# Up projections as Strassen products over pairs of chunks, with prepared weights kept in DRAM

## Time and profile before

| | |
|---|---|
| median of 3 runs | 1947.38 us (1946.74 to 1948.69) |
| the profiled execution's own time | 1943.46 us |
| its span in the trace | 1941.6 us |
| PE busy | 1844.0 us (95% of the span), 8256 matmuls |
| DVE, ACT, POOL busy | 1040.9 us (54%), 523.4 us (27%), 347.8 us (18%) |
| mean granted TensorE clock | 0.99 |
| moved by DMA | 66.39 MB, mean 34 GB/s |

### The profile page before, as it was taken

The page is one execution under the profiler, slowest core; times in us unless marked ns, Lnnn a source line. Parts: engine busy times, 40 slices in busy tenths (PEclk is TensorE's granted clock), DMA queues, the critical chain, the costliest instruction groups (busy, mean ns, idle before and its releaser), DMA issues.

```text
span 1941.6 us, 21968 instructions
## 1 busy us (share of the span) xinstructions
PE 1844.0 (95%) x8256; PEld 1513.5 (78%) x8256; DVE 1040.9 (54%) x1598; ACT 523.4 (27%) x833; POOL 347.8 (18%) x318
## 2 busy tenths in 40 slices
PE   6799999999999999999999999999999788899998
PEld 5578888888887888788888888887777566677876
DVE  7653333333336565633333333367566579966676
ACT  4322112111214432321211121133333223322221
POOL 1100000000003110000000000002455462145464
PEclk9899999999999999999999999999999998999999
DMA  7400000000000000001000001000011000000002
GB/s 260 156 1 33 33 33 32 0 32 32 27 5 1 1 1 1 33 33 33 19 14 32 32 4 39 32 33 3 32 44 38 23 33 1 33 34 34 17 34 88
DMA packets 34754, 66.39 MB, mean 34 GB/s; under 512 B 2160, under 2 KB 10736, under 8 KB 32752
## 3 DMA queue, kind: packets, MB, share of 16 engines
q1 hardware_dynamic: 26224, 61.04, 8.7%
...
## 4 chain that ended last, share of the span: by engine, by line
PE 76%; DVE 11%; issue 5%; POOL 5%; ACT 2%; DMA 0%; DVEq 0%; POOLq 0%; SPq 0%; ACTq 0%
PE work L313 18%; PE work L315 18%; PE work L317 13%; PE acc L313 9%; PE acc L317 9%; PE acc L315 7%; POOL x L989 3%; DVE stats L1075 1%; PE work L451 1%; DVE xT_lo L1156 1%; DVE w_lo L1217 1%; DVE hid L1171 1%; DVE waiting L1130 1%; DVE scaled L1194 1%; ACT hid_hi L774 1%
## 5 line engine op out<-in xcount | busy, mean ns | idle before, releaser
L313 PE MATMUL work<-xT_hi,w_hi 128*128 128x512 f32 (+1 forms) x1760 | 692.2, 393 | 26.0 <-issue 10.8
L315 PE MATMUL work<-xT_lo,w_hi 128*128 128x512 f32 (+1 forms) x1760 | 688.6, 391 | 0.0
L317 PE MATMUL work<-xT_hi,w_lo 128*128 (+1 forms) x1056 | 412.6, 391 | 0.0
L313 PEld LDWEIGHTS work<-xT_hi,w_hi 128*128 128x128 f32 x1760 | 332.4, 189 | 97.6 <-issue 18.1
L313 PE MATMUL acc<-w_hi,hid_hi 128*128 128x512 f32 x936 | 370.8, 396 | 25.8 <-DVE scaled L1194 11.7
L315 PEld LDWEIGHTS work<-xT_lo,w_hi 128*128 128x128 f32 x1760 | 332.4, 189 | 71.6 <-issue 3.4
L1171 DVE SCALAR_TENSOR_TENSOR hid<-work,hid 128x512 f32<-128x512 f32 x128 | 88.5, 692 | 532.0 <-ACT hid L771 532.0
L317 PE MATMUL acc<-w_hi,hid_lo 128*128 128x512 f32 x936 | 366.6, 392 | 0.0
L989 POOL TENSOR_TENSOR x<-x,scaled 128x512 f32<-128x512 f32 x188 | 264.4, 1439 | 204.7 <-DVE scaled L1194 168.9
L771 ACT ACTIVATE hid<-work 128x512 f32<-128x512 f32 x128 | 76.6, 598 | 717.2 <-PE work L317 717.2
L1174 DVE TENSOR_TENSOR hid_lo<-hid,hid_hi 128x512 fp32r<-128x512 f32 x216 | 183.3, 849 | 151.0 <-ACT hid_hi L774 151.0
...
## 6 DMA issues: line engine op xcount, KB each, us to landing
...
```

Of the source, the lines that this page charges most:

```text
L313: pe.matmul(out, a_hi, b_hi, start=start, stop=False, skip_group_check=onto)
L315: last = pe.matmul(out, a_hi, b_lo, start=False, stop=stop and zero == "a", skip_group_check=onto)
L317: last = pe.matmul(out, a_lo, b_hi, start=False, stop=stop, skip_group_check=onto)
```

## The change

The up projections work on a pair of chunks (1024 tokens) at a time. For a **unit** (one block of gate rows and one of linear rows; for S the two blocks of B), the 2x2 product of [gate; up] x [two halves of the features] with [two halves] x [two chunks] is formed from seven products instead of eight, in the variant of Strassen's method with shared sums. Each product is two feature slices x three matmuls (two if exact). Names: p1, p5, p6, p2, p7, p3, p4, in PE's order; five PSUM banks hold BX, BY, BZ, BW and BV, and three (`RING`) take turns for down products and transposes.

- The sums on the weights' side (`w13_sums`) are made and split once, in pass 0 for A and in pass 1 for B and S, written to DRAM (`w13_kept`, 1.84 MB a unit; `w2_kept`, 0.52 MB a block) and loaded by SP for each unit from pass 1 on.
- The sums on the tokens' side (`sums`, four) and their split into seven operands (`convert`) are made once for each pass. `xc_hi` and `xc_lo` exist once: an operand is converted when the last unit of the pass before has used it.
- The sums behind the products go through PSUM: ACT copies BX to BY (`seed_y`) before p6 adds to it, ACT keeps p5 in SBUF (`keep_p5`), DVE writes BZ = BY + p5 (`seed_z`) before p3, ACT copies BY to BW after p7 (`seed` of BW, in ACT's slot) before p4, DVE writes BV = BY + p5 (`sum_c22`).
- The outer loop is over ten **passes** (layer, pair of chunks), and inside over units, called slots (`run`). Down products of a group stand between the first four and the last three products of the one or two slots after it; those of the last group (eight tiles) stand alone behind the last unit, in `tail`.
- B's down products are summed in SBUF (`y`) by DVE, not by GpSimd. The last group adds onto banks that ACT has filled with `y` (`seed`), DVE scales them, and `finish` adds them to x at the start of the pass after. The S layer's D * x moves from DVE and PSUM to GpSimd.
- One flag, read once before the first B pass, decides for all B passes. No engine's program has loops.

```diff
--- before.py
+++ after.py
...
+PASSES = [("A", 0, 0), ("A", 0, 1), ("A", 2, 0), ("A", 2, 1), ("B", 3, 0), ("B", 3, 1),
+          ("S", 4, 0), ("S", 4, 1), ("B", 5, 0), ("B", 5, 1)]
...
+W_OF = {"p1": 1, "p5": 3, "p6": 4, "p2": 2, "p7": 5, "p3": 6, "p4": 0}
+X_OF = {"p1": 0, "p5": 1, "p6": 2, "p2": 3, "p7": 4, "p3": 5, "p4": 6}
+
+BX, BY, BZ, BW, BV, RING = 0, 1, 2, 3, 4, 5
...
+    w13_kept = nc.dram_tensor("w13_kept", [W13_BASE["S"] + 1, P, 2 * 7 * 2 * P], F32).ap()
...
+            def w13_load(ps, s):
+                u = ps.u0 + s
...
+                if u >= 2:
+                    sp.wait_ge(p4_done, u - 1)
+                sp.dma_start(w13[:, u % 2, :, :].rearrange("p a n -> p (a n)").bitcast(F32),
+                             w13_kept[W13_BASE[ps.kind] + s]).then_inc(w13_in[u % 2], 16)
...
+            def prepared_out(s):
+                n = UNITS["A"] + s
+                sp.wait_ge(w13_ready, n + 1)
+                if s + 1 < UNITS["B"]:
+                    flat_load(t["gate"][s + 1], t["up"][s + 1])
+                elif s < UNITS["B"]:
+                    flat_load(t["b"][0], t["b"][1])
+                sp.dma_start(w13_kept[n], prep13[:, :, :].rearrange("p a n -> p (a n)").bitcast(F32)).then_inc(kept13[n % 2], 16)
...
-            def up(w, pair, c, buf, b, matrices, exact=False):
-                pair_wait(w)
-                for m in range(matrices):
-                    for k in range(KD):
-                        at = slice(b * D + k * P, b * D + (k + 1) * P)
-                        last = three(pe, work[:, 2 * pair + m, :], w_hi[buf][:, m, at], w_lo[buf][:, m, at],
-                                     xT_hi[:, c, k, :], xT_lo[:, c, k, :], k == 0, k == KD - 1,
-                                     "a" if exact else None)
-                last.then_inc(pair_full, 1)
...
+            def product(u, name, b, start, exact, first, done):
+                if first is not None:
+                    pe.wait_ge(xc_ready, conv_done(first) + X_OF[name] + 1)
+                for k in range(2):
+                    ws = slice((2 * W_OF[name] + k) * P, (2 * W_OF[name] + k + 1) * P)
+                    last = three(pe, bank(b), w13[:, u % 2, 0, ws], w13[:, u % 2, 1, ws], xc_hi[:, X_OF[name], k, :],
+                                 xc_lo[:, X_OF[name], k, :], start and k == 0, k == 1, "a" if exact else None, not start)
+                last.then_inc(done, 1)
...
+            def first_half(ps, s, exact):
+                u, first = ps.u0 + s, ps if s == 0 else None
+                if ps.no == 0:
+                    pe.wait_ge(w13_ready, s + 1)
+                else:
+                    pe.wait_ge(w13_in[u % 2], nth(u - passes[1].u0, 2))
+                if ps.no == BEFORE_T and s == 0:
+                    pe.wait_ge(t_free, len(t_use))
+                if u:
+                    pe.wait_ge(c11_read, u)
+                else:
+                    pe.wait_ge(fw_out, 16)
+                product(u, "p1", BX, True, exact, first, p1_done)
+                if u:
+                    pe.wait_ge(c22_read, u)
+                if ps.no == BEFORE_T and s == 0:
+                    pe.wait_ge(att_added, CH * TT)
+                if u == 0:
+                    pe.wait_ge(turned, PT)
+                product(u, "p5", BV, True, exact, first, p5_done)
+                pe.wait_ge(y_seeded, u + 1)
+                product(u, "p6", BY, False, exact, first, p6_done)
+                product(u, "p2", BX, False, exact, first, p2_done)
...
+            def second_half(ps, s, exact):
+                u, first = ps.u0 + s, ps if s == 0 else None
+                pe.wait_ge(z_seeded, u + 1)
+                product(u, "p7", BY, False, exact, first, p7_done)
+                product(u, "p3", BZ, False, exact, first, p3_done)
+                pe.wait_ge(w_seeded, u + 1)
+                product(u, "p4", BW, False, exact, first, p4_done)
...
+                onto = ps.kind == "B" and g == len(ps.groups) - 1
+                if onto:
+                    pe.wait_ge(seeded, PT * {3: 0, 5: 2}[ps.li] + PT * ps.pair + i + 1)
+                else:
+                    bank_free("d", d)
...
+            def run(ps, exact=False):
+                for s in range(ps.n):
+                    first_half(ps, s, exact)
+                    for g, i, d in ps.downs[s]:
+                        down(ps, g, i, d, exact)
+                    turn_tiles(ps, s)
+                    second_half(ps, s, exact)
+                for g, i, d in ps.downs[ps.n]:
+                    down(ps, g, i, d, exact)
+                turn_tiles(ps, ps.n)
...
+            def convert(ps, m):
+                act.wait_ge(sums_ready, 4 * (ps.no + 1))
...
+                else:
+                    act.wait_ge(freeing[m], ps.u0)
+                copy(xc_hi[:, m, :, :], sources[m], AF.Copy).then_inc(xc_hi_ready, 1)
...
+            def seed_y(u):
+                act.wait_ge(p1_done, u + 1)
+                if u:
+                    act.wait_ge(c22_ready, u)
+                copy(bank(BY), bank(BX), AF.Copy).then_inc(y_seeded, 1)
...
+            def keep_p5(u):
+                act.wait_ge(p5_done, u + 1)
+                if u:
+                    act.wait_ge(hid_ready, plan.lo_no[u - 1, 0, 1])
+                copy(sg[:, 1, :], bank(BV), AF.Copy).then_inc(p5_kept, 1)
...
+            def seed(ps, i, d):
+                user = plan.free_by["d", d]
+                act.wait_ge(freed[user[0]], user[1] + 1)
+                act.wait_ge(added, d - PT + 1)
+                copy(bank(plan.ring["d", d]), y[:, i, :], AF.Copy).then_inc(seeded, 1)
...
+            def tail(ps):
+                following, m = follower(ps), 4
+                for g, i, d in ps.downs[ps.n]:
+                    if ps.kind == "B":
+                        seed(ps, i, d)
+                    if following and m < 7:
+                        convert(following, m)
+                        m += 1
...
+            def sums(ps, step):
+                b11, b12, b21, b22, t2 = (xs[:, n, :, :] for n in range(5))
+                if step == 0:
+                    dve.wait_ge(turned, turns_before(ps.no + 1))
+                    tt(b12, b22, b12, ALU.subtract).then_inc(sums_ready, 1)
+                elif step == 1:
+                    dve.wait_ge(sums_ready, 4 * ps.no + 1)
+                    tt(t2, b12, b11, ALU.add).then_inc(sums_ready, 1)
+                elif step == 2:
+                    dve.wait_ge(sums_ready, 4 * ps.no + 2)
+                    if ps.no == 6:
+                        dve.wait_ge(skip_done, PT)
+                    tt(xn[:, 0:2, :], b22, t2, ALU.subtract).then_inc(sums_ready, 1)
+                else:
+                    tt(xn[:, 2:4, :], b21, t2, ALU.subtract).then_inc(sums_ready, 1)
...
+            def w13_sums(n):
+                dve.wait_ge(flat_in, 32 * (n + 1))
+                link(tt(flat[:, 4, :], flat[:, 0, :], flat[:, 1, :], ALU.add))
+                tt(flat[:, 6, :], flat[:, 2, :], flat[:, 0, :], ALU.subtract)
+                link(tt(flat[:, 5, :], flat[:, 4, :], flat[:, 2, :], ALU.subtract))
+                tt(flat[:, 7, :], flat[:, 3, :], flat[:, 5, :], ALU.subtract).then_inc(flat_ready, 1)
...
+            def seed_z(u):
+                dve.wait_ge(p6_done, u + 1)
+                dve.wait_ge(p5_kept, u + 1)
+                if u:
+                    dve.wait_ge(c12_read, u)
+                tt(bank(BZ), bank(BY), sg[:, 1, :], ALU.add).then_inc(z_seeded, 1)
...
+            def sum_c22(u):
+                dve.wait_ge(w_seeded, u + 1)
+                tt(bank(BV), bank(BY), sg[:, 1, :], ALU.add).then_inc(c22_ready, 1)
...
+            def gated(ps, s):
+                u = ps.u0 + s
+                scale = up_s[:, s:s + 1] if ps.kind == "B" else 1.0
+                dve.wait_ge(c12_read, u + 1)
+                dve.wait_ge(c22_ready, u + 1)
+                nc.vector.scalar_tensor_tensor(sg[:, 1, :], bank(BV), scale, sg[:, 1, :], ALU.mult,
+                                               ALU.mult).then_inc(c22_read, 1)
+                dve.wait_ge(c11_read, u + 1)
+                dve.wait_ge(p4_done, u + 1)
+                nc.vector.scalar_tensor_tensor(sg[:, 0, :], bank(BW), scale, sg[:, 0, :], ALU.mult,
+                                               ALU.mult).then_inc(c21_read, 1)
+                low(u, 0, 1, sg[:, 1, :])
+                low(u, 0, 0, sg[:, 0, :])
...
+            def slot(ps, s):
+                u, following, last = ps.u0 + s, follower(ps), ps.no == len(passes) - 1
+                seed_z(u)
+                if ps.no == 0 and s + 1 < UNITS["A"]:
+                    w13_split(s + 1)
+                if s == 0:
+                    finish(ps)
+                m = 0
+                for g, i, d in ps.downs[s]:
+                    add_tile(ps, g, i, d)
+                    if following and s == ps.n - 1:
+                        convert(following, m)
+                        m += 1
+                if ps.no == 0:
```

(48 more changed lines are left out.)

1932 lines of the change are left out of this document (993 added, 939 removed).

## The result

The changed kernel takes 1983.29 us (median of 4 runs, 1979.9 to 1987.43), the kernel before in the same session 1947.06. The ratio is 1.0186, 95% interval 1.0164 to 1.0208: 36 us slower. The forecast was 1959, 12 us slower, with a range that holds the result.

The account below looks back on a forecast made before the run. PE was taken to set the time. New costs less old waits, 141 us, against 130 saved gave +11: 1955 on the profiled 1943.46, and 1959 us as median. Range 1895 to 2010, the forecast's own 1940 to 1990.

Parts of the forecast that it names:

- What was removed: Up projections in A, B and S: 572 fewer matmuls at 0.2267 us each, 129.7 us saved.
- The wait in a B unit: Exact B: p6 starts 4.4 us after p7's end, matmuls cover 3.63; 0.75 us per unit, 33 us over 44.
- The rival in which this chain closes: B units: p7's end to p6 takes 3.6 us or less, B's 33 us go, total 1926; chance 0.34.
- Ends of passes: Last down tiles stand uncovered behind the last unit: 14 us over four A passes, 32 us in B.
- S: The two S passes: open chain, DVE's queue and cold restarts leave PE idle, 54 us.
- start: Before pass 0's first product: p1 at 102 us instead of 85.1, +17 us, bounds 8 and 25.
- starts of passes: First slots: statistics on DVE ahead of `seed_z`, also weight sums and first operands in pass 0; A 8 us, B 22.
- the section on waits in a unit: Chain from p7 to the next unit's p6: no wait in A, where 24 matmuls take 5.44 us; 33 us in B.
- transfers: Pass 1's loads and stores just fit beside PE at 398 GB/s; 5 us taken for the 12 units.
- the rival in which transfers bound pass 1: Pass 1: at 300 GB/s a unit takes 18.3 us instead of 15.2, total 1991; chance 0.10.
- restarts: After long idle gaps in S, PE restarts at the 1.2 GHz clock: four gaps, 7 us, inside S's 54.
- attention priced at +4: Attention: conversions for pass 2 behind the last attended tile, 2.3 us, and last softmax without transposes to fill it, 2.

Follow-up runs that it names:

- no_seeds: Changed kernel without the three copies that carry partial sums between PSUM banks, so outputs lack those sums: 1929.47 us, ratio 0.9909.
- p7_split: Changed kernel with p7 behind two of a slot's down tiles instead of four, DVE and ACT orders adapted: 1995.35 us, ratio 1.0248.
- combined2: Changed kernel with many queue reorderings from single runs together, plus repairs to pass 1's attention tiles and B's second statistics: 1914.74 us, ratio 0.9827.
- pass_ends: Changed kernel with two instead of four of DVE's input conversions ahead of a pass's last C22 sum, the others later: 1976.85 us, ratio 1.0138.
- flat_first: Changed kernel with SP, in pass 0, issuing the next raw up weights' load ahead of the wait for W2's split: 1967.59 us, ratio 1.0102.
- no_affine: Changed kernel without three of ACT's four scaling operations per tile transposed in pass 1, so attention's inputs lack them: 1974.87 us, ratio 1.0134.
- warm_fill: Changed kernel with 396 added matmuls that nobody reads filling PE's longest waits, no order changed: 1977.79 us, ratio 1.0150.

## Why the prediction was wrong in size

**What was removed** is right to the matmul: 7684 at a distance of 0.2267 us.

**The wait in a B unit** is right in mechanism and close in size. PE, ACT and DVE around one:

```profile
1409.43 0.39 PE L357 MATMUL psum<-xc_hi,w 128*128 128x512 f32 x1
1409.63 0.58 ACT L950 ACTIVATE psum<-psum 128x512 f32<-128x512 f32 x1 [3.85 <-PE psum L359]
...
1410.46 0.69 DVE L1323 TENSOR_TENSOR psum<-psum,sg 128x512 f32<-128x512 f32 x1
...
1411.25 0.69 ACT L953 ACTIVATE sg<-psum,small 128x512 f32<-128x512 f32 x1 [1.04 <-DVE psum L1323]
...
1411.97 0.75 DVE L1330 SCALAR_TENSOR_TENSOR sg<-psum,small,sg 128x512 f32<-128x512 f32 x1 [0.82 <-ACT sg L953]
...
1412.78 0.50 PE L357 MATMUL psum<-xc_hi,w 128*128 128x512 f32 x1 [0.42 <-DVE sg L1330]
...
1413.93 0.50 PE L357 MATMUL psum<-xc_hi,w 128*128 128x512 f32 x1
```

p7's slot is over at 1409.43. The copy from PSUM to PSUM takes 0.58 us (0.60 taken), p5 starts after 3.35 us, p6 after 4.50 (4.4 forecast) where 16 matmuls take 3.63. A slot is 10.8 us without other work on DVE and 11.0 with an input sum, for 10.75 forecast. The rival in which this chain closes needed 0.75 us less; with the seeds gone (no_seeds) or p7 earlier (p7_split, combined2) it does close, so the rival named the right lever.

**Ends of passes.** Before the B tails PE waits 6.09 us (6.2 forecast), in A 3.8, 2.7, 3.1, 3.1 (3.4). pass_ends shows the cause, DVE's conversions.

**S** is 51 us for 54, its waits 10.3, 13.2, 5.6, 3.6, 8.2 and 1.5 for 10.8, 12.9, 5.4, 6.1, 7.7 and 3.9. The **start** was too dear by 5 us.

**The first step that failed: the weight preparation of pass 0 priced at nothing but its first slots.** The term "starts of passes" gave pass 0 3.1 us for statistics and weight sums and 1.2 for first operands, and the section on waits in a unit said of A "no wait". That compared the length of one chain with PE's work. It did not follow the queues: of the extra 26 us, flat_first returns 13 (16 in the total) by issuing one load earlier. The other 12 or so stay open: in flat_first's pass 0 PE still has waits of 3.3, 2.8 and 1.3 us on DVE in its first slots. PE was held by an add, which was behind a split, which was behind ACT's split, which was behind a load, which was behind SP's wait for something else. SP's program shows this order before anything runs; each DMA of a moved step has to be placed in time against the wait in front of it.

**The second: pass 1's slots with attention tiles.** The term for it held 5 us for transfers and 3 for DVE. Transfers cost next to nothing. From 400 to 540 us:

```profile
400.00:540.00 140.00, 140.00 (x610) 113.55 (x609) 99.04 (x150) 78.68 (x120) 0.00 (x0) 1.00 0.93 364
```

PE is busy without a gap at a DMA share of 0.93 (0.9 forecast) and 364 GB/s, and the slots are 15.2 us. The 364 GB/s are 2% above the figure of 358 GB/s that the Trainium skill's page DMA: Bandwidth & Descriptors, under Specifications, gives for a core; the rival in which transfers bound pass 1 is refuted. The 0.2 us above the 15.0 of passes 2 and 3 are a hand-over at C22's gate (starts 0.29 and 0.34 us apart in place of 0.23), not a load. What was missed is ACT: two tiles a slot with 4.1 us of scaling and splitting in front of the seed of W, 1.2 to 1.5 us of wait in each of five slots (no_affine: 8 us).

**The third: restarts.** The forecast put 7 us for the lower clock, in S alone. The rows that are 0.43 us apart add up to 39.0 us for 14.0 before: they stand behind long waits at the ends and starts of passes and in attention too, most at 1.2 to 2.6 us apiece. warm_fill got 10 of them back. Beside that, the short waits cost more than they show: of the 1.0 us that a B slot of 11.0 is too long, the rows show 0.42 as wait; the rest is the first matmul after it, the hand-over to p6 and matmuls begun late.

**The fourth: attention priced at +4.** It lost 16. The forecast had the two ends: the wait for the first conversion is 2.1 us (2.3 taken), the last softmax wait 1.5 (2 taken). It had nothing for the start and the middle. PE's recorded waits, without the one for the conversion, are 17.4 us for 7.3 before: 5.1 and 0.5 for the first softmax, 4.2 twice for the second norm's output (L886), 3.4 for low parts, the 1.5 among them. Before the first softmax stands, once more, other work in DVE's queue, four statistics of 2.46 us in all ahead of the causal mask (L1505) whose scores wait:

```profile
663.31 2.46 DVE L1208 BATCH_NORM_STATS2 stats<-x 128x6 f32<-128x512 f32 x4
...
666.10 0.27 DVE L1505 TENSOR_TENSOR psum<-psum,causal 128x128 f32<-128x128 f32 x1
...
667.43 0.47 PE L655 MATMUL psum<-ident,sg 128*128 128x128 f32 x1 [5.10 <-ACT sg L1017]
```

No run moves them, so what they cost is not shown.

**And an error the other way, which is luck.** The prediction took the waits of the kernel before as length less PE busy: 3 us in the A layers and 50 in B and S. But a matmul is busy for 0.39 us at a distance of 0.2267, so the busy time hides part of each wait behind it. Measured as in the table, by distance, the same layers lose 7 and 77 us: the first B layer's window in the earlier trace rows is 296 us with 1088 products and 72 transposes, 42 us of loss where the prediction reads 29. So the change took away 84 us of old waits and not 53. With the same terms and this value the sum would have come to 1928 us, faster than before. The new terms add up to 255 us where 197 were forecast, 58 too few; the old waits gave 31 back and the end took 3, which leaves the 30 us between 1955 and the profiled 1984.6.

Of the 58, pass 0 has +26, pass 1 +12, attention +12, the B passes +17 and passes 2 and 3 +6; the start and S are 5 and 3 us better than forecast, and the 5 us of branches lie inside the passes. The restarts, +18, are not beside these but within them (5 us in pass 0).
